# Two softmax attentions of a five-stage kernel: scores in groups of 32 rows, turns in two halves, one bank for q, k and v, norms by four tiles, mask by sixteen

## The chip, the cores and the metric

The kernel runs on one NeuronCore of a Trainium2 chip. Its time is the device time of one launch in microseconds. Before the change the median of three runs is 3300.31 us (3300.05 to 3302.07). The engines are PE (matrix multiply, with its weight loads shown apart as PEld), DVE (VectorE), ACT (ScalarE), POOL (GpSimd) and SP, which issues most DMAs.

## The reference

The input x is 128 sequences of 64 tokens of width 128, with a context of the same shape. A stack of four gated cross-attention blocks follows, each with a feed-forward; all data is float32. The change touches two of the attentions, both multi-head softmax attentions with 16 heads of width 8:

```
x^ = layernorm(x);  q = x^ Wq + bq;  k = ctx Wk + bk;  v = ctx Wv + bv
scores[h] = q[h] k[h]^T / sqrt(8)          64 x 64 per sequence and head
layer 1 alone: padded keys and keys after the query are masked out
x = x + (softmax(scores) v) Wo + bias
```

The others (a lag-correlation attention, a retention, integer, gated and expert-routed feed-forwards and attentions) are left as they are.

## The kernel before

Two sequences make a tile of 128 tokens, so there are 64 tiles. x stays in SBUF as X[128, 64, 128], and the transposed context as CT. `program` runs the stages one after another: weights; the first attention with its feed-forward; `softmax_attention` for layer 1; the next feed-forward; retention; the gated feed-forward; `softmax_attention` for layer 3, which also stores x to DRAM; and last the expert-routed stage (`switch_attention`), which takes more than half of the time and is not touched.

Inside `softmax_attention` each engine has its own instruction list, written out for all tiles by `straight(stages, bufs)`: at step t every stage (lag, function) works on tile t - lag, in the order of the list. That order is the engine's program order, and semaphores hold the engines together. SBUF buffers rotate over NS = 4 tiles; the eight PSUM banks do not rotate, so each is written again only when it was read. A tile passes through these steps:

- DVE takes the moments of its 128 rows (L217, L220), adds epsilon (L223); POOL raises to the power -1/2 (L236); DVE normalises (L244, `norm`).
- PE turns x (`turn_x`, L1165), ACT keeps it (L1088). PE projects q, k and v (`project`, L1150 to L1155): q and k in one bank, v in another. ACT keeps q and k with their biases (L1079, L1082). DVE spreads v over a block-wise layout (`widen` of DVE, L1043).
- POOL spreads the key (`widen` of POOL, L985): with 16 heads of 8 rows, `key_wide` holds for each of 8 heads of a half the key with all other heads' rows set to zero. So one matmul with 64 contraction rows gives the scores of 8 heads: 64 queries by 8 x 64 keys.
- PE makes the scores (`scores`, L1139): 2 halves of heads by 2 sequences are four matmuls of 64 rows, 64 columns and 512 moving columns, two banks in all.
- Layer 1: DVE builds the tile's mask row (L1016), adds it to the scores (L1022), takes the row maximum (L1031), and POOL subtracts it (`centre`, L979). Layer 3: DVE takes the maximum straight from PSUM (L1026) and subtracts it (L1036).
- ACT exponentiates (L1073). PE turns the probabilities (`turn_probs`, L1129), eight transposes into two banks; ACT keeps them in one instruction (L1069). PE weighs the values (`weigh`, L1118), DVE divides by the row sum (L1006, L1010), PE turns the heads (L1107), ACT keeps them, PE makes the output (L1100), and DVE adds it to x (L1002).

PE's list is: turn heads, output, project, turn probabilities, weigh, turn x, scores. SP fetches the tile's context from CT into a buffer of four (L956), SBUF to SBUF, and in layer 3 stores x (L960). In layer 1 SP first loads the causal mask and the padding mask, and DVE waits for both before anything else but four small copies.

## Time and profile before

| what | value |
|---|---|
| median of the runs | 3300.31 us |
| the profiled execution, its own time | 3297.7 us |
| its span, first to last instruction | 3295.9 us |
| mean granted TensorE clock | 0.923 |
| busy share of PE, DVE, ACT, POOL | 89%, 85%, 71%, 70% |
| layer 1's attention, first to last instruction | about 233 to 561 us |
| layer 3's attention | about 1010 to 1325 us |
| expert-routed stage with its weights | from about 1327 us to the end |

The busy shares are means over stages with different limits. The page's slices give the outline, the busy times of chosen stretches tell which engine is full in each, and the timeline of one step tells why. A matmul in float32 leaves two records.

### The profile page before, as it was taken

The numbers are of one execution on the slowest core, as the hardware profiler recorded it, in microseconds if no ns is written. First come the engines' busy times: TensorE is split into PE (matmuls) and PEld (weight loads), VectorE is DVE, ScalarE is ACT, GpSimd is POOL, SyncE is SP. The second block draws the span as 40 slices with busy tenths as digits, with TensorE's granted clock in tenths as the row PEclk, the third lists the DMA queues.
The fourth block names the chain that finished last, engine by engine and source line by source line (L and its number), as shares of the span: only waits on it lengthen the run. The fifth ranks groups of instructions, "written<-read, shape, count | busy, mean of one in ns | idle before, by whom it ended". The sixth has DMA issues, their size and how long they took to land.

```text
span 3295.9 us, 78554 instructions
## 1 busy us (share of the span) xinstructions
PE 2947.3 (89%) x24633; PEld 2207.1 (67%) x24646; DVE 2792.6 (85%) x9096; ACT 2344.1 (71%) x7533; POOL 2305.8 (70%) x3108
## 2 busy tenths in 40 slices
PE   6639997289668999399999999999999999999998
PEld 6526775167345777277777777777777777777776
DVE  4369997599897998588999989898989999898987
ACT  3276665777896666477777777777777777777776
POOL 1179996564686665167777777777777777777777
PEclk8559998599678999699999999999999999999999
DMA  3000000022000100400000000000000000000000
GB/s 111 15 12 16 16 17 7 21 73 71 1 1 21 31 29 27 124 8 8 7 9 9 8 7 9 9 8 9 7 8 9 7 7 8 9 8 7 8 8 5
DMA packets 132959, 63.73 MB, mean 19 GB/s; under 512 B 20417, under 2 KB 132161, under 8 KB 132545
## 3 DMA queue, kind: packets, MB, share of 16 engines
q1 hardware_dynamic: 132544, 58.70, 6.4%
q8 instruction: 200, 3.28, 0.4%
q14 instruction: 215, 1.75, 0.2%
HBM read 41.82 MB, written 8.45 MB: 15 GB/s over the span
## 4 chain that ended last, share of the span: by engine, by line
PE 57%; POOL 0%; DVE 0%; ACT 0%; issue 0%; DMA 0%; POOLq 0%; SPq 0%; DVEq 0%; ACTq 0%
PE ps_sw_a L2127 23%; PE ps_sw_d L2127 22%; PE ps_sw_w L2169 4%; PE ps_sw_w L2156 3%; PE ps_sw_s L2142 2%; PE ps_sw_s L2180 2%; PE ps_sw_m L2147 1%; PE ps_sw_m L2135 0%; ACT sw_scaled L1915 0%; POOL sw_o_rest L1881 0%; POOL sw_o_rest L1878 0%; DVE sw_v_part L2029 0%; ACT sw_probs L1964 0%; DMA sw_x<-scratch_x 0%; DVE sw_r_sel L2044 0%
## 5 line engine op out<-in xcount | busy, mean ns | idle before, releaser
L1915 ACT ACTIVATE sw_scaled<-ps_sw_a,sw_gate_o 128x128 f32<-128x128 f32 x2048 | 620.5, 447 | 252.3 <-PE ps_sw_a L2127 244.3
L1915 ACT ACTIVATE sw_scaled<-ps_sw_a,sw_gate_v 128x128 f32<-128x128 f32 x2048 | 597.7, 450 | 203.3 <-PE ps_sw_a L2127 203.2
L2029 DVE SCALAR_TENSOR_TENSOR sw_o_part<-ps_sw_d,sw_gate_o,sw_o_part 128x128 f32<-128x128 f32 x1920 | 555.1, 338 | 60.6 <-PE ps_sw_d L2127 59.5
L1854 POOL TENSOR_TENSOR sw_v_pair<-sw_v_part,sw_scaled 128x256 f32<-128x256 f32 x512 | 378.2, 739 | 158.8 <-DVE sw_v_part L2029 101.7
L2029 DVE SCALAR_TENSOR_TENSOR sw_v_part<-ps_sw_d,sw_gate_v,sw_scaled 128x128 f32<-128x128 f32 x1024 | 304.8, 338 | 123.1 <-PE ps_sw_d L2127 104.3
L1878 POOL TENSOR_TENSOR sw_o_rest<-sw_o_rest,sw_scaled 128x256 f32<-128x256 f32 x384 | 285.3, 743 | 155.2 <-ACT sw_scaled L1915 117.9
L2029 DVE SCALAR_TENSOR_TENSOR sw_v_part<-ps_sw_d,sw_gate_v,sw_v_part 128x128 f32<-128x128 f32 x1024 | 304.5, 338 | 0.0
L1881 POOL TENSOR_TENSOR sw_o_rest<-sw_o_rest,sw_scaled 128x256 f32<-128x256 f32 x384 | 282.7, 736 | 30.1
L1859 POOL TENSOR_TENSOR sw_v<-sw_v_pair 128x128 f32<-128x128 f32 x512 | 241.7, 472 | 40.1
L985 POOL TENSOR_TENSOR at_key_wide<-at_keyT,c_half_heads 128x1024 f32<-128x1024 f32 x128 | 242.5, 1895 | 4.2 <-ACT at_keyT L1082 4.2
L2127 PE MATMUL ps_sw_a<-sw_v_high,sw_xT_high 128*128 128x512 f32 x512 | 235.6, 460 | 0.4 <-ACT sw_scaled L1915 0.3
L2127 PE MATMUL ps_sw_a<-sw_o_high,sw_ctx_high 128*128 128x512 f32 x512 | 214.6, 419 | 0.6 <-ACT sw_scaled L1915 0.6
L2127 PE MATMUL ps_sw_d<-sw_v_high,sw_xT_high 128*128 128x512 f32 x512 | 208.0, 406 | 0.0
L2127 PE MATMUL ps_sw_d<-sw_o_high,sw_ctx_high 128*128 128x512 f32 x512 | 207.2, 405 | 0.0
L2127 PE MATMUL ps_sw_d<-sw_v_low,sw_xT_high 128*128 128x512 f32 x512 | 203.0, 396 | 0.0
L2127 PE MATMUL ps_sw_a<-sw_v_low,sw_xT_high 128*128 128x512 f32 x512 | 202.7, 396 | 0.0
L2127 PE MATMUL ps_sw_a<-sw_v_high,sw_xT_low 128*128 128x512 f32 x512 | 202.3, 395 | 0.0
L2127 PE MATMUL ps_sw_d<-sw_v_high,sw_xT_low 128*128 128x512 f32 x512 | 201.9, 394 | 0.0
L2127 PE MATMUL ps_sw_a<-sw_o_low,sw_ctx_high 128*128 128x512 f32 x512 | 201.8, 394 | 0.0
L2127 PE MATMUL ps_sw_d<-sw_o_low,sw_ctx_high 128*128 128x512 f32 x512 | 201.5, 393 | 0.0
L2127 PE MATMUL ps_sw_a<-sw_o_high,sw_ctx_low 128*128 128x512 f32 x512 | 200.3, 391 | 0.0
L2127 PE MATMUL ps_sw_d<-sw_o_high,sw_ctx_low 128*128 128x512 f32 x512 | 200.3, 391 | 0.0
(326 smaller groups left out, 8582.1 us busy)
## 6 DMA issues: line engine op xcount, KB each, us to landing
at_ctxT<-ctx_T SPq DMA_DIRECT2D x128, 64.0 KB, 1.8
re_values<-in_ctx SPq DMA_DIRECT2D x128, 64.0 KB, 2.4
x<-in_x SPq DMA_DIRECT2D x16, 256.0 KB, 3.4
l_ctx<-in_ctx SPq DMA_DIRECT2D x16, 256.0 KB, 3.0
re_ctx<-in_ctx SPq DMA_DIRECT2D x16, 256.0 KB, 3.1
scratch_x<-x SPq DMA_DIRECT2D x64, 64.0 KB, 1.8
swp_staged<-in_L_ffn_v_w SPq DMA_DIRECT2D x8, 512.0 KB, 5.9
swp_staged<-in_L_ffn_o_w SPq DMA_DIRECT2D x8, 512.0 KB, 7.1
```

What stands on the lines that cost most here:

```text
L985: pool.tensor_tensor(key_wide[:, s], keyT[:, s].unsqueeze(1).broadcast_to([P, HALF, P]), C["half_heads"][:].unsqueeze(2).broadcast_to([P, ...
L1854: pool.tensor_tensor(v_pair[:, h % 2], v_part[:, h], scaled[:, h % 4, 2:4], ALU.add)\
L1859: pool.tensor_tensor(v[:, h], v_pair[:, h % 2, 0], v_pair[:, h % 2, 1], ALU.add).then_inc(q["v"], 1)
L1878: pool.tensor_tensor(o_rest[:, 0:2], o_rest[:, 0:2], scaled[:, h % 4, 0:2], ALU.add)\
L1881: pool.tensor_tensor(o_rest[:, 2:4], o_rest[:, 2:4], scaled[:, h % 4, 2:4], ALU.add)\
L1915: act.activation(scaled[:, h % 4, e], ps_a[h % 2][:, e], ACT.Copy, scale=gates[:, s, h, HALF_E + e:HALF_E + e + 1]).then_inc(a_scaled[kind ...
L2029: dve.scalar_tensor_tensor(out=acc[:, e % 2], in0=ps_d[h % 2][:, e], scalar=gates[:, s, h, e:e + 1], in1=before, op0=ALU.mult, op1=ALU.add ...
L2127: m = pe.matmul(bank, lhs[a], w[b][:, h, experts], start=c == 0, stop=c == 2)
L2142: m = pe.matmul(ps_s[t, h], probs[t, s, h], C["ident"][t, t], start=True, stop=True)
L2156: m = pe.matmul(ps_w[n][:, h * P:(h + 1) * P], W["pair"][:, 4 * n + h], xT[:, s], start=True, stop=True)
L2169: m = pe.matmul(ps_w[b][:, h * S:(h + 1) * S], v[t, h], probs_T[t, h], start=True, stop=True)
L2180: m = pe.matmul(ps_s[t], xT[:, s, t], uT[:, :, t], start=True, stop=True)
```

## The change

`softmax_attention` is written anew in these points, for both layers; the retention is not changed.

- A new constant `quarter_heads`; `key_wide` holds 4 heads' keys in place of 8. Scores are eight matmuls of 32 rows, 64 columns and 256 moving columns. Each group of 32 rows has a bank of its own, half used, so scores take four banks.
- The probabilities are turned in two halves of four transposes through one bank: first half, `weigh` of the tile before, second half. ACT keeps each half with its own instruction.
- q, k and v share one bank; DVE places the values after the key was kept.
- The norm's small steps are done once for four tiles, and the normalisation is an ACT instruction with scale and bias.
- The mask of layer 1 is built for 16 tiles at a time, and only that step waits for the masks' loads.
- The context is read from CT directly, and its fetches are gone.
- Lags grow by five steps for scores and what follows them.

```diff
-    for name, shape in (("ident", [P, P]), ("half_heads", [P, HEADS // 2]), ("half_mask", [P, 2])):
+    for name, shape in (("ident", [P, P]), ("half_heads", [P, HEADS // 2]),
+                        ("quarter_heads", [P, HEADS // 4]), ("half_mask", [P, 2])):
...
-        ctxT = k.sb(name + "_ctxT", [P, NS, P])
-        key_wide = k.sb(name + "_key_wide", [P, NS, HALF, P])
+        key_wide = k.sb(name + "_key_wide", [P, NS, QUARTER, P])
-        ps_s = k.psum(name + "_scores", [P, HEADS, S])
-        ps_t = k.psum(name + "_turned", [P, HALF, P])
+        ps_s = k.psum(name + "_scores", [P, 4, 512])[:, :, 0:QUARTER * S].rearrange("p r (j s) -> p r j s", j=QUARTER)
+        ps_t = k.psum(name + "_turned", [P, HALF // 2, P])
         ps_a = k.psum(name + "_a", [P, 2, P])
-        ps_qk = k.psum(name + "_qk", [P, 2, P])
-        ps_v = k.psum(name + "_v", [P, P])
+        ps_qkv = k.psum(name + "_qkv", [P, 3, P])
+        ps_v = ps_qkv[:, 2]
...
-                def fetch(i, s, r):
-                    if not first(i, NS):
-                        sp.wait_ge(q["proj"], i - NS + 1)
-                    sp.dma_start(ctxT[:, s], tile_of(CT, i)).then_inc(ctx_in[s], 16)
... POOL
-                stages = [(5, centre)] if masked else []
-                straight(stages + [(1, add_bias), (0, rstd), (3, widen)], NS)
+                stages = [(10, centre)] if masked else []
+                straight(stages + [(7, add_bias), (1, by_group(rstd)), (8, widen)], NS)
... DVE
-                if masked:
-                    dve.wait_ge(q["consts"], 48)
+                def build_mask(i, s, r):
+                    if i % CHUNK == 0:
+                        if i == 0:
+                            dve.wait_ge(q["consts"], 48)
+                        dve.scalar_tensor_tensor(out=mask[:, i:i + CHUNK], in0=padding[:, i:i + CHUNK], scalar=NEG,
+                                                 in1=causal[:].unsqueeze(1).broadcast_to([P, CHUNK, S]),
+                                                 op0=ALU.mult, op1=ALU.min).then_inc(q["mask"], 1)
...
+                def place_values(i, s, r):
                     dve.wait_ge(q["proj"], i + 1)
+                    dve.wait_ge(q["keyT"], i + 1)
...
+                def negated_mean(g, s):
+                    dve.wait_ge(q["rstd"], g + 1)
+                    if g >= 4:
+                        dve.wait_ge(q["xhat"], N * (g - 3))
+                    dve.scalar_tensor_tensor(out=small["nmr"][:, s], in0=mv[:, s, :, 0], scalar=-1.0, in1=small["rstd"][:, s],
+                                             op0=ALU.mult, op1=ALU.mult).then_inc(q["nmr"], 1)
...
-                straight([(5, read_scores), (9, final), (5, centre), (1, norm), (0, front), (3, widen), (7, normalise)], NS)
+                stages = [(10, read_scores), (14, final), (10, centre), (2, by_group(negated_mean)), (0, moments),
+                          (1, aggregate), (1, by_group(variance)), (8, place_values), (12, normalise)]
+                straight(([(7, build_mask)] if masked else []) + stages, NS)
... ACT
+                def norm(i, s, r):
+                    act.wait_ge(q["nmr"], i // N + 1)
...
+                    act.activation(xhat[:, s], X[:, i], ACT.Identity, bias=small["nmr"][:, g, i % N:i % N + 1],
+                                   scale=small["rstd"][:, g, i % N:i % N + 1]).then_inc(q["xhat"], 1)
...
-                straight([(8, keep_heads), (3, keep_q), (6, keep_probs), (2, keep_x), (5, exp)], NS)
+                straight([(13, keep_heads), (8, keep_q), (11, keep_probs(0)), (6, norm), (11, keep_probs(1)), (7, keep_x),
+                          (10, exp)], NS)
... PE
-                    for half in range(2):
-                        h = slice(half * S, (half + 1) * S)
-                        for b in range(2):
-                            t = slice(b * S, (b + 1) * S)
-                            m = pe.matmul(ps_s[t, half * HALF:(half + 1) * HALF], qT[h, s, t], key_wide[h, s, :, t],
-                                          start=True, stop=True)
+                    for b in range(2):
+                        t = slice(b * S, (b + 1) * S)
+                        for quarter in range(4):
+                            h = slice(quarter * ROWS, (quarter + 1) * ROWS)
+                            m = pe.matmul(ps_s[t, quarter], qT[h, s, t], key_wide[h, s, :, t], start=True, stop=True)
...
-                straight([(8, turn_heads), (9, output), (3, project), (6, turn_probs), (7, weigh), (2, turn_x),
-                               (4, scores)], NS)
+                straight([(13, turn_heads), (14, output), (8, project), (11, turn_probs(0)), (12, weigh), (11, turn_probs(1)),
+                          (7, turn_x), (9, scores)], NS)
```

## Rows read from the trace of the kernel before

**Rows 1.** The page: PE's busy share in 40 equal slices, in tenths.

```profile
PE   6639997289668999399999999999999999999998
```

**Rows 2.** Stretches of layer 1 and 3: length, each engine's busy us, clock, DMA.

```profile
core 0: us, PE busy (x) PEld busy (x) DVE busy (x) ACT busy (x) POOL busy (x), PEclk, DMA share, GB/s
249.00:544.00 295.00, 290.89 (x3939) 206.26 (x3935) 282.81 (x671) 194.13 (x370) 290.95 (x247) 0.99 0.05 15
1018.50:1311.00 292.50, 290.71 (x3940) 207.00 (x3943) 261.86 (x609) 194.97 (x373) 178.15 (x184) 0.99 0.10 29
```

**Rows 3.** Timeline of a step of layer 3: start, us, engine, line, operation.

```profile
...
1149.80 1.23 DVE L1026 TENSOR_REDUCE at_top<-ps_at_scores 128x16 f32<-128x1024 f32 x1 [0.31 <-PE ps_at_scores L1139]
...
1150.98 1.09 PE L1129 MATMUL ps_at_turned<-c_ident,at_probs 128*128 128x128 f32 x8
...
1151.38 0.36 ACT L1082 ACTIVATE at_keyT<-ps_at_qk,w_bk 128x128 f32<-128x128 f32 x1
...
1152.27 0.34 DVE L244 TENSOR_SCALAR at_xhat<-x,at_mv,at_rstd 128x128 f32<-128x128 f32 x1
...
1153.06 0.15 DVE L223 TENSOR_SCALAR at_var<-at_mv 128x1 f32<-128x1 f32 x1
...
1153.31 1.09 PE L1139 MATMUL ps_at_scores<-at_key_wide,at_qT 64*64 64x512 f32 x8
...
1153.81 1.90 POOL L985 TENSOR_TENSOR at_key_wide<-at_keyT,c_half_heads 128x1024 f32<-128x1024 f32 x1
1153.86 0.29 DVE L1010 TENSOR_TENSOR at_heads_out<-ps_at_o,at_rsum 128x128 f32<-128x128 f32 x1
...
1154.33 0.33 PE L1107 MATMUL ps_at_a<-c_ident,at_heads_out 128*128 128x128 f32 x1
...
1154.46 1.23 DVE L1026 TENSOR_REDUCE at_top<-ps_at_scores 128x16 f32<-128x1024 f32 x1 [0.31 <-PE ps_at_scores L1139]
```

**Rows 4.** Timeline of a step of layer 1.

```profile
...
400.02 0.14 PEld L1107 LDWEIGHTS ps_at_a<-c_ident,at_heads_out 128*128 128x128 f32 x1 [0.81 <-DVE at_heads_out L1010]
...
400.33 1.23 DVE L1022 TENSOR_TENSOR at_raw<-ps_at_scores,at_mask 128x1024 f32<-128x1024 f32 x1
...
401.67 1.21 DVE L1031 TENSOR_REDUCE at_top<-at_raw 128x16 f32<-128x1024 f32 x1
...
402.97 1.93 POOL L979 TENSOR_TENSOR at_probs<-at_raw,at_top 128x1024 f32<-128x1024 f32 x1
...
404.70 0.14 PEld L1107 LDWEIGHTS ps_at_a<-c_ident,at_heads_out 128*128 128x128 f32 x1 [0.81 <-DVE at_heads_out L1010]
...
406.04 1.09 PE L1129 MATMUL ps_at_turned<-c_ident,at_probs 128*128 128x128 f32 x8
```

**Rows 5.** Timeline in retention: its score matmuls and the load behind them.

```profile
...
705.24 1.11 PE L1404 MATMUL ps_re_s<-re_q_wide,re_kT 64*64 64x256 f32 x16
...
706.27 1.01 PEld L1389 LDWEIGHTS ps_re_o<-re_val_wide,re_probs 128*64 128x64 f32 x32 [0.39 <-issue]
```

**Rows 6.** Single tiles of other stages: line, count: ns min/median/max, first and last start.

```profile
L1349 ACT ACTIVATE re_xhat<-x,re_nmr,re_rstd x64: 477/481/495, 647.6 to 800.2; 128x128 f32<-128x128 f32 x64
L1296 DVE SCALAR_TENSOR_TENSOR re_nmr<-re_mv,re_rstd x16: 794/1366/1643, 646.8 to 797.5; 128x4 f32<-128x4 f32 x16
...
L1272 POOL TENSOR_TENSOR re_rstd<-re_var,minus_half x16: 1017/1017/1019, 645.7 to 796.1; 128x4 f32<-128x4 f32 x16
...
L321 DVE SCALAR_TENSOR_TENSOR l_nmr<-l_mv,l_rstd x16: 151/162/164, 39.8 to 101.7; 128x4 f32<-128x4 f32 x16
...
L372 ACT ACTIVATE l_xT<-ps_l_x x16: 572/597/597, 44.1 to 112.4; 128x512 f32<-128x512 f32 x16
```

**Rows 7.** The mask row of layer 1, all 64, in the same view.

```profile
L1016 DVE SCALAR_TENSOR_TENSOR at_mask<-at_padding,at_causal x64: 214/476/1004, 249.4 to 544.3; 128x64 f32<-128x64 uint8 x64
```

**Rows 8.** Timeline: the kernel's start and the start of layer 1.

```profile
...
2.58 0.43 SPq L164 DMA_DIRECT2D gates_raw<-in_g_ffn  x1
...
240.44 0.29 DVE L217 BATCH_NORM_STATS2 at_stats<-x 128x6 f32<-128x128 f32 x1 [7.18 <-DMA at_padding<-in_mask_BxS_bf]
...
248.65 1.99 PE L1139 MATMUL ps_at_scores<-at_key_wide,at_qT 64*64 64x512 f32 x8
```

More of the change, by code:

```diff
@@ L938, in softmax_attention, with by_group, at, by_rows @@
         out_ps = ps_o[:, 256:256 + D]
-        q = k.sems(name, *LN_SEMS, "consts", "ctx_read", "x_turned", "xT", "proj", "qT", "keyT", "key", "val", "ones",
-                   "scores", "mask", "masked", "top", "centred", "exp", "p_turned", "p_kept", "pv", "rsum",
-                   "heads", "h_turned", "h_kept", "out", "x", "biased", "stored")
-        ctx_in = [k.sem(f"{name}_ctx_in{n}") for n in range(NS)]
+        q = k.sems(name, "stats", "moments", "var_eps", "rstd", "nmr", "xhat", "consts", "x_turned", "xT", "proj", "qT", "keyT",
+                   "key", "val", "ones", "scores", "mask", "masked", "top", "centred", "exp", "p_turned", "p_kept", "pv",
+                   "rsum", "heads", "h_turned", "h_kept", "out", "x", "biased", "stored")
+        def by_group(step):
+            def at(i, s, r):
+                if i % N == N - 1:
+                    step(i // N, i // N % 4)
+            return at
+        def by_rows(ap):
+            return ap.rearrange("p (r j) s -> p r j s", r=4)
+        def head_wide(ap):
+            return ap.rearrange("p (r j) -> p r j", r=4).unsqueeze(3).broadcast_to([P, 4, QUARTER, S])
         with nc.Block() as block:
@@ L961, in store @@
                         .then_inc(q["stored"], 16)
-                straight([(0, fetch)] + ([(10, store)] if out is not None else []), NS)
                 if out is not None:
+                    straight([(0, store)], NS)
                     sp.wait_ge(q["stored"], 16 * TILES)
@@ L976, in centre @@
                     pool.wait_ge(q["top"], i + 1)
-                    if not first(i, NS):
-                        pool.wait_ge(q["p_turned"], i - NS + 1)
+                    if i >= NS:
+                        pool.wait_ge(q["p_turned"], 2 * (i - NS + 1))
                     pool.tensor_tensor(probs[:, s], raw[:, s], top[:, s].unsqueeze(2).broadcast_to([P, HEADS, S]),
@@ L1007, in normalise @@
                     dve.wait_ge(q["rsum"], i + 1)
-                    if not first(i, NS):
+                    if i >= NS:
                         dve.wait_ge(q["h_turned"], i - NS + 1)
@@ L1109, in weigh @@
                 def weigh(i, s, r):
-                    pe.wait_ge(q["p_kept"], i + 1)
+                    pe.wait_ge(q["p_kept"], 2 * i + 2)
                     pe.wait_ge(q["val"], i + 1)
-                    if not first(i, 2):
+                    if i >= 2:
                         pe.wait_ge(q["x"], i - 1)
@@ L1122, in weigh, with turn_probs, step @@
                     m.then_inc(q["pv"], 1)
[L1124 to L1140 removed]
+                def turn_probs(part):
+                    def step(i, s, r):
+                        pe.wait_ge(q["exp"], i + 1)
+                        if 2 * i + part:
+                            pe.wait_ge(q["p_kept"], 2 * i + part)
+                        for n in range(HALF // 2):
+                            j = part * HALF // 2 + n
+                            m = pe.transpose(ps_t[:, n], probs[:, s, 2 * j:2 * j + 2].rearrange("p h k -> p (h k)"),
+                                             C["ident"][:])
+                        m.then_inc(q["p_turned"], 1)
+                    return step
+                def scores(i, s, r):
+                    pe.wait_ge(q["key"], i + 1)
+                    pe.wait_ge(q["qT"], i + 1)
+                    if i:
+                        pe.wait_ge(q["masked" if masked else "centred"], i)
+                    for b in range(2):
[3 more added lines that the diff above has]
+                            m = pe.matmul(ps_s[t, quarter], qT[h, s, t], key_wide[h, s, :, t], start=True, stop=True)
                     m.then_inc(q["scores"], 1)
@@ L1144, in project @@
                     pe.wait_ge(q["xT"], i + 1)
-                    pe.wait_ge(ctx_in[s], 16 * r + 16)
-                    if not first(i, 1):
+                    if i:
                         pe.wait_ge(q["qT"], i)
@@ L1149, in project @@
                         pe.wait_ge(q["val"], i)
-                    pe.matmul(ps_qk[:, 0], W["q"][:], xT[:, s], start=True, stop=True)
-                    pe.matmul(ps_qk[:, 1], W["k"][:], ctxT[:, s], start=True, stop=True)
+                    pe.matmul(ps_qkv[:, 0], W["q"][:], xT[:, s], start=True, stop=True)
+                    pe.matmul(ps_qkv[:, 1], W["k"][:], CT[:, i], start=True, stop=True)
                     for parity in range(2):
```

124 lines of the change are left out of this document (66 added, 58 removed).

## The prediction

> **What bounds the kernel now.** The page of the profile comes first: its slices say that PE is full in two stretches which are no part of the last stage, the fourth to sixth slice and the fourteenth to sixteenth [rows 1]. The code puts the softmax attentions of layers 1 and 3 there. The stretches' busy times confirm it: PE 98.6% and 99.4% at the full clock (0.99 of 2.4 GHz), and in layer 1 DVE is at 96% and POOL at 99% too [rows 2]. ACT is at 66%. Then one step of the timeline for each attention, since a step repeats unchanged some 60 times.
>
> Layer 3 [rows 3]: DVE's row maximum starts at 1149.80 and again at 1154.46, so a step is 4.66 us. PE runs without a gap: the turns of the probabilities at 1150.98, scores at 1153.31, next turn of heads at 1154.33. Scores occupy it 1.02 us. DVE begins 0.13 us after PE's scores make way (1154.46 against 1154.33) and ends its last operation at 1153.86 + 0.29 = 1154.15, before PE wants it. PE alone sets this step.
>
> Layer 1 [rows 4]: 404.70 - 400.02 = 4.68 us. Here three bounds meet. PE has the same work. DVE has no gap. And there is a chain: scores read at 400.33, centred by POOL from 402.97, turned on PE at 406.04, which is 5.71 us from the read to the turn and crosses a step.
>
> **The change part by part.** I call the step of layer 3 T3, that of layer 1 T1, and count 61 steady steps of each (64 tiles less filling).
>
> Scores. Four matmuls of 64 rows, 64 columns and 512 moving columns become eight of 32 rows and 256 columns. One matmul is two records of about 0.61 us; four quadrants go side by side and the whole takes 1.02 us. The trace has no 32-row tile. The nearest rows are retention's: 64x64 tiles, 256 columns, 16 records from 705.24 to the next load at 706.27, so 1.03 us for eight matmuls, four at a time [rows 5]. Upper bound 1.03 if no more than four run together, lower bound half of it, 0.51, if eight do. I take 0.51 plus 0.1 for eight more records to issue, 0.61, since four and two column halves already share the array here and only the number of row groups is new. PE's step becomes 4.66 - 1.02 + 0.61 = 4.25 us.
> The Trainium skill, TensorEngine Tiling (Array Packing), lists 32x64 among its modes with eight tiles, under Tiling Modes. The same page, Performance Considerations, warns that tiling speeds up TensorE and not PSUM's evacuation. By the one, 0.51; by the other the readers of PSUM are next, which is where the following terms end up.
>
> Key widening on POOL: half the elements. It is 1.90 us for 1024 now [rows 3]. Between a half (0.95) and all of it I take 1.04, the half and some fixed cost. In layer 3 it is hidden (POOL is busy 178 of 292 us [rows 2]). In layer 1 it takes POOL off its bound: about 4.62 a step, less 0.86, less the grouped power.
>
> Norms by four tiles. DVE loses the normalisation (0.34, of which 0.3 is not overlapped) and the one-column addition (0.15) [rows 3]. Per group it gets an addition (0.15 again) and the negated mean (0.16 alone [rows 6]). POOL's power, now once a tile, becomes 1.02 per four tiles [rows 6]. ACT gets the normalisation at 0.48 [rows 6]. DVE in layer 3: 1154.15 - 1149.80 = 4.35, less 0.45, makes 3.90; with 0.13 of semaphore at each end 4.16, under PE's 4.25, so it hides, with only 0.09 to spare. In the group's step it is 4.16 + 0.31 = 4.47, plus what the negated mean waits for POOL. In retention this instruction takes 1.37 us in the median against 0.16 elsewhere [rows 6]: it reads two SBUF tensors while POOL works. In layer 3 POOL's widening (1.04) runs from about 2.1 to 3.1 us of the step and the negated mean arrives at 2.6, so 0.5 more at worst. That is 0.22 to 0.72 lost per four steps; with a step of every four I take 0.4, or 0.10 a tile. T3 = 4.35.
>
> Turns in two halves, one bank. PE's work is the same eight transposes. The second half waits for ACT to clear the first, and `weigh` of the tile before lies between, about 1.0 us (2.33 from the turns' start to scores, less the turns' 1.0 and the turn of x, 0.3 [rows 3]). An eviction of 512 columns is 0.60 us [rows 6], so two are 1.20 in place of 1.02. ACT takes query and key first, the key from 1151.38 to 1151.74 or 2.1 us into PE's step (which began at 1149.67, 4.66 before 1154.33) [rows 3], then the half until 2.6; PE asks at 1.3 + 0.5 + 1.0 = 2.8 or a little later. The cover is 0.2 to 0.3 us; gone, every step pays what it lacks. Behind the waiting turn stand turn of x and scores. ACT in all: 195 / 292.5 x 4.66 = 3.1, plus 0.48, plus 0.18 = 3.8, under the step.
>
> q, k and v in one bank, with values placed after the key is kept: DVE reaches the values at about 3 us, the key is kept at 2.1, so it costs nothing. The fetch DMAs go and with them a transfer per tile on SP's queue. PE has no gap in the step that could be a wait for one, so this too is worth nothing.
>
> The chain of layer 1. DVE no longer builds a mask row between, so the read starts 0.13 after PE's scores and not 0.31. Read to turn stays 5.71. From the turn to the end of scores PE needs 1153.31 - 1150.98 = 2.33 plus 0.61. The loop spans two steps: (0.13 + 5.71 + 2.33 + 0.61) / 2 = 4.39. This is later than PE's 4.25, so the chain through POOL's centring is what is late next. With 0.04 for group steps T1 = 4.43.
>
> Mask by sixteen. It was 0.48 per tile in the median, 0.21 at least and 1.00 at most [rows 7]: again two SBUF inputs against POOL. 1024 elements at the rate of DVE's other 1024 forms is 1.2 us; at the worst, in proportion to 0.21 for 64, it is 3.4. Three of the four chunks fall into steady steps and stand before the read of scores. With a wait for POOL's operation, 1.3 each, 4 us in all; bounds 0 and 10.
>
> Filling. In layer 1 DVE waited 7.18 us for the padding mask before its first statistics at 240.44 (0.29 each) [rows 8]. Now statistics begin at once and only the mask at lag 7 waits. Five statistics steps of 0.5, the power 1.0, norm, turn, project and the wait for the constants until 240.4, then the mask's 1.2: first scores near 244.2, where they were at 248.65 [rows 8]. Gain 4.4. In layer 3 there was no such wait and the five steps cost about 3, against 1.9 saved by the smaller widening and the lost stalls: 0.6 later. Draining through two half turns costs 0.5 in layer 1, nothing sure in layer 3. One more constant on SP's queue: 0.47 between issues (last at 2.58 [rows 8]), ahead of everything: 0.5.
>
> **The sum.** Layer 3: 61 x (4.66 - 4.35) = 18.9, less 0.6, 18.3. Layer 1: 61 x (4.68 - 4.43) = 15.3, less 4, plus 4.4, less 0.5, 15.2. Constants -0.5. Together 33.0 us. The profiled execution took 3297.7 (span 3295.9) and would take 3264.7; the median shown is 2.6 above it, so 3267.3.
>
> **The rivals.** About 0.2%, 6.6 us, is what can be told from no change here.
> (B) Better: the group step's excess is absorbed and eight tiles cost 0.51. T3 = 4.20, T1 = 4.36: 9 + 4 more, 3254. For it: DVE's operations overlap by nearly 0.1 each. Against: only 0.09 of slack.
> (C) No more than four matmuls run at once, as retention's rows show for eight: scores 1.03, both steps stay near 4.67 and only the ends count: 0.6 - 0.6 + 4.4 - 4 - 0.5 - 0.6 - 0.5, about 3302. Retention's tiles are limited to four by shape, so they don't decide it.
> (D) The negated mean loses to POOL's centring in layer 1. Both wait for the row maximum. If POOL is first, DVE stands for 1.93: that group step is 4.16 + 0.31 + 1.93 = 6.4, 2.0 over, 0.5 a tile, T1 = 4.93. Layer 1 then loses 15.3 + 0.1, layer 3 with 1.04 of wait per group (T3 = 4.48) gains 10.4: 3306. It decides from a wait of about 1 us on. For it: retention's 1.37. Against: DVE issues it behind its own maximum, with no semaphore between, and POOL starts 0.09 later (402.97 against 401.67 + 1.21 [rows 4]).
> The Trainium skill, SBUF — State Buffer, section on its two separate sides, calls this pair of ports an exclusive lock held for the whole instruction by the first to start. The retention row agrees (0.79 to 1.64 against 0.16), and by it the result hangs on who is first, as in (D).
> (E) The other side: the four row groups don't run beside each other, only the two column halves. Then four rounds of 0.51 are 2.04, PE's step is 5.68, and 2 x 61 x 1.02 = 124 us are added: 3425. It decides as soon as scores pass 1.1 us. Against: two row groups do run together in both traces' rows.
>
> **Chances.** Forecast 0.66, B 0.14, C 0.07, D 0.08, E 0.05. Faster by over 0.2%: forecast, B and a mild D, 0.82. Within 0.2%: half of C and D, 0.09. Slower 0.09. The range leaves out E, the worst of D and C and the best of B: 3248 to 3298, where the unknown costs (scores 0.51 to 1.03, mask 0 to 10, group steps 0.22 to 0.72) put most of their weight.
>
> **What would show it.** Scores: 16 records of 32 rows in about 0.6 us, next turn of heads 4.25 to 4.4 later. DVE without idle time in layer 3. In layer 1 ACT's exponential following POOL's centring at once, and PE waiting for it at the first half turn. Negated mean under 0.7 us in the median. First scores of layer 1 near 244. The prediction is wrong if PE idles at the second half turn (the cover was not there), if scores take over 0.8, or if the mask chunks take over 2 us.

## The result

The changed kernel takes 3308.14 us (median of 12 runs, 3303.77 to 3312.29) against 3300.33 us before (12 runs, 3290.80 to 3304.69). The ratio is 1.0023, with a 95% interval from 1.0016 to 1.0031. The forecast was 3267.3 with a range up to 3298: it was wrong in sign and outside its range. The profiled execution has a span of 3305.2 us, 9.3 more than before, where the prediction's own sum was 33.0 less.

The page's slices, then the busy times of the two stretches in the profile after (they answer to [rows 1] and [rows 2]):

```profile
PE   6649997289667999499999999999999999999998
...
249.00:544.00 295.00, 270.88 (x4316) 207.94 (x4315) 249.92 (x499) 213.64 (x482) 218.55 (x198) 0.97 0.01 2
1018.50:1311.00 292.50, 275.62 (x4358) 211.10 (x4359) 237.59 (x511) 210.16 (x494) 107.38 (x143) 0.96 0.05 15
```

No engine is full now. In layer 3 PE falls from 290.7 to 275.6 us of 292.5, DVE from 261.9 to 237.6, POOL from 178.2 to 107.4. The work did shrink as forecast, and the time didn't: it has turned into waits. The timeline of one step tells which. Layer 3, PE from one scores to the next, and then the two copies of ACT on which PE's wait hangs (they answer to [rows 3]; columns as there):

```profile
...
1165.30 0.66 PE L1179 MATMUL ps_at_turned<-c_ident,at_probs 128*128 128x128 f32 x4
1165.79 0.27 PE L1217 MATMUL ps_at_a<-c_ident,at_xhat 128*128 128x128 f32 x1
1166.00 0.69 PE L1193 MATMUL ps_at_scores<-at_key_wide,at_qT 32*64 32x256 f32 x16
1166.90 0.30 PE L1155 MATMUL ps_at_a<-c_ident,at_heads_out 128*128 128x128 f32 x1 [0.22 <-ACT at_xT L1135]
```

```profile
...
1165.99 0.60 ACT L1114 ACTIVATE at_probs_T<-ps_at_turned 128x512 f32<-128x512 f32 x1 [0.65 <-PE ps_at_turned L1179]
1166.49 0.27 ACT L1135 ACTIVATE at_xT<-ps_at_a 128x128 f32<-128x128 f32 x1
```

The turn of heads starts 0.90 us after the scores and not 0.61, because it waits for the copy of the turned x. `turn_heads` has always had that wait in the code (both turns use one bank). Before, ACT copied x right after its turn, under scores of 1.02 us (they ran from 1153.31 to 1154.33 [rows 3]):

```profile
...
1153.42 0.28 ACT L1088 ACTIVATE at_xT<-ps_at_a 128x128 f32<-128x128 f32 x1 [0.28 <-PE ps_at_a L1165]
```

Now ACT takes the second half of the turned probabilities first (`straight([... keep_probs(1)), (7, keep_x) ...])`), stands for it until 1165.99, and gives x only at 1166.76, while scores have become short. The steps in layer 3 are 4.59 us, with 4.75 to 4.77 in nine of them. This is **cause B** below.

In layer 1 three steps of four are 4.59 too; the fourth is 5.29. DVE's part of such a step:

```profile
...
321.38 0.17 DVE L1082 BATCH_NORM_AGGREGATE at_mv<-at_stats 128x2 f32<-128x6 f32 x1
321.58 1.69 DVE L1086 TENSOR_SCALAR at_var<-at_mv 128x4 f32<-128x4 f32 x1
323.19 0.41 DVE L1065 TENSOR_TENSOR at_val_wide<-ps_at_qkv,c_half_mask 128x256 f32<-128x256 f32 x1
...
323.80 0.29 DVE L1032 TENSOR_TENSOR at_heads_out<-ps_at_o,at_rsum 128x128 f32<-128x128 f32 x1
```

GpSimd's centring in that step, and PE:

```profile
...
321.35 1.90 POOL L994 TENSOR_TENSOR at_probs<-at_raw,at_top 128x1024 f32<-128x1024 f32 x1 [0.79 <-DVE at_top L1052]
```

```profile
...
322.62 0.69 PE L1193 MATMUL ps_at_scores<-at_key_wide,at_qT 32*64 32x256 f32 x16
324.14 0.33 PE L1155 MATMUL ps_at_a<-c_ident,at_heads_out 128*128 128x128 f32 x1 [0.84 <-DVE at_heads_out L1032]
```

The group's addition of epsilon over four columns lasts 1.69 us, until GpSimd's centring ends (323.27 and 323.25). The values, the reciprocal and the division of the heads stand behind it in DVE's list, and PE idles 0.84 us. The group's small operations in all steady steps, layer 1 first, then layer 3 (line, count: ns min/median/max):

```profile
L1086 DVE TENSOR_SCALAR at_var<-at_mv x14: 1689/1689/1881, 261.9 to 513.1; 128x4 f32<-128x4 f32 x14
...
L1074 DVE SCALAR_TENSOR_TENSOR at_nmr<-at_mv,at_rstd x14: 149/152/154, 268.5 to 518.2; 128x4 f32<-128x4 f32 x14
...
L1086 DVE TENSOR_SCALAR at_var<-at_mv x13: 169/170/171, 1058.7 to 1280.3; 128x4 f32<-128x4 f32 x13
...
L1074 DVE SCALAR_TENSOR_TENSOR at_nmr<-at_mv,at_rstd x14: 151/893/922, 1044.5 to 1284.7; 128x4 f32<-128x4 f32 x14
```

Where POOL centres (layer 1) the addition meets it; where POOL only widens (layer 3) the negated mean does, 0.89 us. This is **cause A**.

The start of layer 1 (answers to [rows 8]):

```profile
...
243.23 1.23 DVE L1017 SCALAR_TENSOR_TENSOR at_mask<-at_padding,at_causal 128x1024 f32<-128x1024 uint8 x1 [4.91 <-DMA at_padding<-in_mask_BxS_bf]
...
249.11 1.22 DVE L1042 TENSOR_TENSOR at_raw<-ps_at_scores,at_mask 128x1024 f32<-128x1024 f32 x1 [0.39 <-PE ps_at_scores L1193]
```

The first scores are read 1.67 us earlier than before (250.78), not 3.9. The 9.3 us can be split by the starts of the first and last reads of the scores in both traces: first read of layer 1 -1.7; first to last read in layer 1 294.5 before, 302.9 after, +8.4; on to layer 3's first +0.1; layer 3 291.7 and 291.4, -0.3; the rest +2.7. Forecast were -3.9, -11.3, +1.1, -18.9 and 0. The stretches from first to last read in the two attentions are 38 of the 42 us missed.

### The profile page after: what moved, and what is told of

The parts are those of the page before. It is cut to its first block, busy times and chain, and to the rows that moved or that the text cites. A ratio compares the mean times of both kernels' runs of the same rounds, so it can differ in the third digit from the quotient of the medians.

```text
span 3305.2 us, 80565 instructions
## 1 busy us (share of the span) xinstructions
PE 2922.3 (88%) x25657; PEld 2217.5 (67%) x25670; DVE 2738.2 (83%) x8844; ACT 2392.9 (72%) x7789; POOL 2165.4 (66%) x3012
## 4 chain that ended last, share of the span: by engine, by line
PE 57%; DVE 0%; POOL 0%; ACT 0%; issue 0%; DMA 0%; POOLq 0%; SPq 0%; DVEq 0%; ACTq 0%
PE ps_sw_a L2179 23%; PE ps_sw_d L2179 22%; PE ps_sw_w L2221 4%; PE ps_sw_w L2208 3%; PE ps_sw_s L2194 2%; PE ps_sw_s L2232 2%; PE ps_sw_m L2199 1%; PE ps_sw_m L2187 0%; ACT sw_scaled L1967 0%; DVE sw_v_part L2081 0%; POOL sw_o_rest L1930 0%; POOL sw_o_rest L1933 0%; ACT sw_probs L2016 0%; DMA sw_x<-scratch_x 0%; DVE sw_r_p L2091 0%
## 5 line engine op out<-in xcount | busy, mean ns | idle before, releaser
L1114 ACT ACTIVATE at_probs_T<-ps_at_turned 128x512 f32<-128x512 f32 x256 | 152.9, 597 | 96.9 <-PE ps_at_turned L1179 96.8
L1001 POOL TENSOR_TENSOR at_key_wide<-at_keyT,c_quarter_heads 128x512 f32<-128x512 f32 x128 | 133.2, 1041 | 129.9 <-ACT at_keyT L1129 129.9
```

Of the source, the lines that this page charges most:

```text
L1001: pool.tensor_tensor(key_wide[:, s], keyT[:, s].unsqueeze(1).broadcast_to([P, QUARTER, P]), C["quarter_heads"][:].unsqueeze(2).broadcast_t ...
L1114: act.activation(probs_T[:, s, part * HALF // 2:(part + 1) * HALF // 2], ps_t, ACT.Copy)\
```

## The experiments

Each was timed over five rounds beside the kernel before; ratios are to it, and that of the change is 1.0023. "Layer 1 goes at" and "layer 3 goes at" give the steps from one read of the scores to the next. "4.26/4.53" means that the two alternate.

**1. The epsilon addition at the end of DVE's list.**

```
-                          (1, aggregate), (1, by_group(variance)), (8, place_values), (12, normalise)]
+                          (1, aggregate), (8, place_values), (12, normalise), (1, by_group(variance))]
```

> One edit to the changed kernel: the group's addition of epsilon on DVE (variance) moves from behind the moments to the end of DVE's list. Theory A: in layer 1 this 4-column addition takes 1.70 us because it waits until POOL's centring ends, and it makes every fourth step 5.29 in place of 4.59. At the end of the list it starts about 0.3 to 0.5 us before the centring ends, so it lasts 0.3 to 0.6 us and ends beside DVE's own wait for scores: steps of 5.29 go down to at most 4.75, layer 1 is 8 us shorter (13 x 0.6), layer 3 at most 2 us; total about 3299. Rival: the long step comes from the group's other work (POOL's power of four columns before the widening); then steps stay at 5.29 and the time at 3308.

3300.19 us, 0.9999 (0.9988 to 1.0011), 8 us under the change. Layer 1 goes at 4.59 from its sixth step on, apart from the mask's steps; layer 3 stays at 4.59/4.77. The addition there:

```profile
L1086 DVE TENSOR_SCALAR at_var<-at_mv x14: 159/388/405, 261.9 to 507.6; 128x4 f32<-128x4 f32 x14
```

Cause A is shown, with its price: 13 steps by 0.70 is 9 us. From first to last read layer 1 is only 4.9 us shorter (298.0 against 302.9): in this trace PE's lower clock lasted longer at the start of the layer (granted 0.50 in place of 0.57 from 255 to 270 us), and the fourth and fifth step took 7.12 and 5.78 us in place of 4.84 and 4.59.

**2. The turn of x ahead of the weighing, its copy ahead of the norm.**

```
-                straight([..., (11, turn_probs(0)), (12, weigh), (11, turn_probs(1)), (7, turn_x), (9, scores)], NS)
+                straight([..., (11, turn_probs(0)), (7, turn_x), (12, weigh), (11, turn_probs(1)), (9, scores)], NS)
-                straight([..., (11, keep_probs(0)), (6, norm), (11, keep_probs(1)), (7, keep_x), (10, exp)], NS)
+                straight([..., (11, keep_probs(0)), (7, keep_x), (6, norm), (11, keep_probs(1)), (10, exp)], NS)
```

> One edit to the changed kernel, order alone: PE turns x before it weighs the values (not after the second half turn), and ACT keeps x before the norm and the second half (not after it). Theory B: PE's next turn of heads waits 0.3 us for ACT's copy of x, which stands behind the 0.60 copy of the second half; scores themselves free PE after about 0.6. Then the gap from the scores' start to the next turn of heads falls from 0.90 to 0.6 to 0.65 and the step from 4.59 to about 4.35 unless DVE's values (which wait for the weighing) hold it at 4.45: 122 x 0.14 to 0.24 = 17 to 29 us less, so 3279 to 3291 with group steps unchanged. Rival B2: scores in 32-row tiles occupy PE for 0.9 whatever stands behind them (a switch of tile shape); then the gap stays 0.9 and the time 3308.

3282.70 us, 0.9948 (0.9936 to 0.9961). PE in layer 3:

```profile
...
1164.27 0.69 PE L1193 MATMUL ps_at_scores<-at_key_wide,at_qT 32*64 32x256 f32 x16
1164.89 0.33 PE L1155 MATMUL ps_at_a<-c_ident,at_heads_out 128*128 128x128 f32 x1
```

The wait is gone and scores occupy PE 0.62 us. Layer 3 goes at 4.26, with 4.36 in every fourth: 272.0 us from first to last read in place of 291.4. Layer 1 keeps its 5.28, and three of its steps last 6.07 to 6.11: PE's clock falls there (last section).

**3. Both.** The two edits above together.

> Both edits of the two others together. If A and B are right and independent: 3308 less 8 to 10, less 17 to 29, so 3269 to 3283. If DVE becomes the bound once PE doesn't wait, the sum is smaller than the parts. Rivals as with the two.

3276.78 us, 0.9924 (0.9912 to 0.9937). Layer 1 alternates between 4.26 and 4.53, mean 4.40, where the prediction's chain gave 4.39. But layer 3 worsens to steps of 4.26 to 4.36 with 4.60 in every fourth, mean 4.38: a late addition makes POOL's power late, its widening slides under the negated mean, and that takes 0.89 us each time (0.56 in experiment 2).

**4. The same by layer**: the addition last in layer 1 alone (`if masked`), the early x in both.

> Both moves by layer: the turn of x before the weighing and its copy before the second half of the weights' copies in both layers; the group's epsilon addition last on VectorE in layer 1 alone. Theory (two separate causes, each in its own layer): layer 3 keeps the steps of 4.26 with 4.36 every fourth that it had with the early turn alone, layer 1 the 4.26/4.53 that it had with both moves, so the kernel gives 3276.8 - 64 x (4.41 - 4.31) = about 3270 us. Rival (the late addition doesn't cost layer 3 its 0.1 us a step; something else drifts): the time stays at 3277, and layer 3 shows 4.6 in some steps all the same.

3265.71 us, 0.9894 (0.9878 to 0.9909). It is the fastest of all kernels here, and within 2 us of the forecast. Layer 1 at 4.26/4.53, layer 3 at 4.26/4.36.

**5. Only ACT's list**: `(6, norm), (7, keep_x), (11, keep_probs(1))`, PE's order as in the change.

> Only ScalarE's list is changed: the copy of the turned x goes ahead of the copy of the second half of the turned weights; TensorE's order stays as in the change. Theory (the wait is one of order on ScalarE, not of TensorE's work): turn heads no longer waits 0.22 us, the stretch from the scores' start to it falls from 0.90 to some 0.62 to 0.7, and the layer-3 step from 4.59 to 4.3 to 4.4; but x is turned on TensorE after the second half of the weights, so that its copy now delays that half's copy by a wait for TensorE. If that wait takes the place, layer 3 stays at 4.5 to 4.6 and the time within 3300 to 3308; if the order on ScalarE alone was the matter, about 3283 to 3290. Rival (turn heads is late for TensorE's own reasons, the 32-row scores occupying it for 0.9): no change, 3308, with 0.90 from scores to turn heads.

3284.84 us, 0.9943 (0.9926 to 0.9960). ACT in layer 3:

```profile
...
1161.90 0.28 ACT L1135 ACTIVATE at_xT<-ps_at_a 128x128 f32<-128x128 f32 x1 [0.77 <-PE ps_at_a L1217]
1162.07 0.59 ACT L1114 ACTIVATE at_probs_T<-ps_at_turned 128x512 f32<-128x512 f32 x1
```

The turn of heads is at 1162.41, 0.62 after the scores at 1161.79, and the step 4.26. So cause B is the order of two entries in ACT's list: the second half may wait, x may not.

**6. Scores back to 64 rows in two banks**, with the widening of 1024 elements; the rest as in the change.

```
-                            m = pe.matmul(ps_s[t, quarter], qT[h, s, t], key_wide[h, s, :, t], start=True, stop=True)
+                            m = pe.matmul(ps_8[t, half * HALF:(half + 1) * HALF], qT[h, s, t], key_wide[h, s, :, t],
+                                          start=True, stop=True)
```

> The changed kernel with scores as before: four matmuls of 64 rows and 512 columns in two banks, key widened to 8 heads (1024 elements on POOL), all else of the change kept. By theory B most of the shorter scores are lost in the wait for x's copy, so longer scores fill it: scores' start to next turn of heads 1.02 in place of 0.90, step 4.71 in place of 4.59 in layer 3, 61 x 0.12 = 7 us more there. In layer 1 POOL has 0.86 more work a step (4.4 us of 4.7): same or up to 0.3 a step more. Total 3315 to 3335. Rival (scores occupy PE 0.9 by themselves): the same 0.12, this run doesn't tell it apart; it prices the part. If instead the time falls below 3300, the 32-row tiles themselves are what costs.

3325.78 us, 1.0076 (1.0064 to 1.0089). So the scores' part, with its shorter widening, is worth 17.6 us inside the change, and all other parts together cost 25 against the kernel before. Layer 3 has 4.66 with a pair of 4.93 and 4.96 in every four. One of the group's steps, POOL first, then DVE:

```profile
...
1171.83 1.90 POOL L1002 TENSOR_TENSOR at_key_wide<-at_keyT,c_half_heads 128x1024 f32<-128x1024 f32 x1 [0.26 <-ACT at_keyT L1130]
```

```profile
...
1172.28 1.46 DVE L1075 SCALAR_TENSOR_TENSOR at_nmr<-at_mv,at_rstd 128x4 f32<-128x4 f32 x1
```

The negated mean ends with the widening (1173.73 and 1173.74).

**7. And besides the turns in one piece** (eight transposes, one copy, on top of 6).

> The kernel with 64-row scores in two banks (3325.8 us), and besides the weights are turned in one piece of eight transposes and copied in one instruction, as before the change. Theory (the halves bring a second wait on ScalarE that the turned x stands behind; in one piece the copy of x follows its turn again): the layer-3 steps of 4.93/4.96 in every fourth become 4.66, and the time goes down to 3310 to 3318. Rival (the loss of that kernel against the one before comes from the norms by group and not from the halves): 3322 to 3330, with the 4.9 steps still there.

3321.12 us, 1.0065 (1.0050 to 1.0080), between the two ranges and next to the rival's; the interval overlaps with that of 6, and the 4.92/4.96 are still there. So the halves are not what makes the long steps. That the norms by group do is read from the rows of 6 (1.46 us for the negated mean, 1.69 for the addition in layer 1); no run has long scores without the grouping. Halves against the whole is not settled beyond "within 5 us".

**8. The norms tile by tile**, on top of 2 (epsilon, power and normalising each step, the last on DVE).

> With the early turn of x, the norms go tile by tile as before the change (epsilon addition, power and normalising each step, the normalising on VectorE, 0.481 us); all else as in the change. Theory (VectorE needs the relief of the grouping once TensorE is at 4.25): VectorE carries 3.84 us a step in layer 3 after the change and would carry 3.84 + 0.48 + some 0.25 = 4.55, so layer 3 goes at 4.55 instead of 4.29 (+16 us), layer 1 at 4.6 to 4.7 instead of 4.67 (about 0): 3295 to 3302. Rival (the grouping costs by its own waits what it saves): layer 3 stays at 4.3 to 4.4 and layer 1 goes at 4.4 to 4.5, since the four-column addition that waited for GpSimd is gone: 3268 to 3278.

3274.42 us, 0.9926 (0.9905 to 0.9946). DVE carries 13.7 us more in layer 3 than in experiment 2 (226.7 against 213.0 of the 240 us from 1045), and layer 3 goes at 4.40 (4.28/4.52) and not at 4.55, layer 1 at 4.42 to 4.44. The additions of one column in layer 1:

```profile
L225 DVE TENSOR_SCALAR at_var<-at_mv x57: 152/153/156, 267.8 to 521.6; 128x1 f32<-128x1 f32 x57
```

The rival holds for the sum: grouping as the change does it costs more in waits than it saves (8 us by the medians, with intervals that overlap). The steps say where. In layer 1 the grouping loses (285.5 us from first to last read without it, 299.4 with it, or 297.0 in experiment 5), in layer 3 it gains (4.40 a step without it, 4.29 with it). With the addition last in layer 1 (experiment 4) it gains in both: 281.2 us in layer 1 and 4.29 a step in layer 3.

**9. The mask one tile at a time**, on top of 4: `CHUNK = 1`.

> The kernel of both moves by layer, with the mask built tile by tile (64 additions of 64 columns) instead of sixteen tiles at a time (4 of 1024 columns); TensorE, ScalarE and GpSimd keep their lists. Theory (the mask by sixteen is worth little here, since VectorE has 0.5 us a step free in layer 1: it carries 231.9 us of 278): one more VectorE instruction of 0.2 us a step, hidden, while the three long steps of 14.3 instead of 13.1 us that the chunks bring fall away: 0 to 4 us faster, 3262 to 3266. Rival (as the prediction took it: the mask by sixteen saves VectorE time on the step's path, 4 us in all): 3268 to 3275, layer-1 steps over 4.40.

3275.35 us, 0.9923 (0.9909 to 0.9936), 10 us over experiment 4 by the medians and 3.7 by the spans of the profiled executions. Layer 1 goes at 4.52, with 4.59 in every fourth, where the other alternates between 4.26 and 4.53; from first to last read it takes 286.2 us against 281.2. The mask and the centring that holds it:

```profile
...
329.31 1.90 POOL L994 TENSOR_TENSOR at_probs<-at_raw,at_top 128x1024 f32<-128x1024 f32 x1 [1.20 <-DVE at_top L1052]
...
330.63 0.67 DVE L1017 SCALAR_TENSOR_TENSOR at_mask<-at_padding,at_causal 128x64 f32<-128x64 uint8 x1
...
331.22 1.21 DVE L1042 TENSOR_TENSOR at_raw<-ps_at_scores,at_mask 128x1024 f32<-128x1024 f32 x1
```

My theory (hidden) fell. 64 columns need 0.19 us (the fastest of the 64) and take 0.67 at the median, ending with the centring. Beside the mended lists the mask by sixteen is worth 5.0 us in layer 1. (The prediction's 4 us, which the rival calls a saving, were the cost of the four chunks.)

**10. Mask later, values in eight buffers**, on top of 4: `(9, build_mask)` and `val_wide` eight deep.

> As the kernel with both moves by layer, and besides: the mask is built two places later in VectorE's list (lag 9 instead of 7), and the widened values have eight buffers instead of four. Theory (the slow filling of layer 1 comes from the mask's wait for the padding's transfer, 4.9 us, ahead of the first values on VectorE): the first values and the first four steps come 2 to 4 us earlier, so 2 to 4 us less than the kernel of both moves by layer, all of it ahead of 300 us in the trace. Rival (the filling is set by the halves' handshake at the half clock, not by the mask): no difference, within 1 us.

3269.33 us, 0.9899 (0.9883 to 0.9915): no gain, as the rival had it, but not for its reason. The first scores are read at 241.80 in place of 248.22. Of these 6.4 us the stage ahead, which has the same code, accounts for 4.1 (its last matmuls start at 223.70 and 227.82), so the edit is worth 2.3 there, inside the theory's 2 to 4. Behind the first step the next four are 6.11, 7.01, 7.11 and 5.82, in place of 6.49, 4.72, 4.14 and 4.58, and the last read is at 530.37 against 529.43. The stretches from 240 and from 255 us, experiment 4 first, then this one (columns as in [rows 2]):

```profile
240.00:255.00 15.00, 10.26 (x82) 6.53 (x78) 10.04 (x21) 5.11 (x16) 7.71 (x8) 0.50 0.08 5
255.00:270.00 15.00, 14.18 (x212) 10.50 (x211) 10.19 (x21) 11.10 (x26) 10.51 (x11) 0.85 0.01 3
```

```profile
240.00:255.00 15.00, 13.31 (x112) 8.65 (x111) 11.01 (x20) 7.62 (x21) 9.77 (x9) 0.50 0.00 1
255.00:270.00 15.00, 15.00 (x168) 11.41 (x166) 7.54 (x17) 7.42 (x18) 8.46 (x8) 0.53 0.01 2
```

PE is full from 255 to 270 and does 168 matmul records where the other does 212, since it works at its lower level (1.2 of 2.4 GHz) for longer. That need not come from the edit. Experiments 2 and 11 differ in one instruction alone, read their first scores at 246.78 and 246.49, and were granted 0.87 and 0.61 from 255 to 270 us (third and fourth step 5.22 and 4.47 against 7.01 and 5.58). So one profile of each doesn't show whether the early start or chance made the clock rise later, and the edit's worth is not settled.

**11. The addition in another form**, at its place, on top of 2.

```
-                    dve.tensor_scalar(small["var"][:, s], mv[:, s, :, 1], EPS, None, ALU.add).then_inc(...)
+                    dve.scalar_tensor_tensor(out=small["var"][:, s], in0=mv[:, s, :, 1], scalar=EPS, in1=mv[:, s, :, 1],
+                                             op0=ALU.add, op1=ALU.max).then_inc(...)
```

> With the early turn of x; the group's epsilon addition stays at its place in VectorE's list, but is written as a two-operation instruction on two tensor operands, max(var + epsilon, var), over the same four columns, in place of the tensor-and-scalar form. Theory (it is this form on four strided columns that stands still while GpSimd's centring runs; the negated mean, two tensor operands and four columns, took 0.154 us at the median, and the one-column tensor-and-scalar form 0.15 us beside a centring): the addition takes about 0.16 us, layer 1 goes at 4.26/4.53 (4.40 mean) and layer 3 at 4.26/4.36 (4.29): 3282.7 - 64 x (4.67 - 4.40) = about 3266 us. Rival (the place is the matter, four strided columns wait for GpSimd in any form): the addition stays at 1.7 us, steps of 5.28 in every fourth, 3283 us.

3285.31 us, 0.9955 (0.9940 to 0.9970): the theory of the form fell. Its premise was weak: the negated mean, which has this form too, already stood for 0.89 us beside the widening in layer 3.

```profile
L1086 DVE SCALAR_TENSOR_TENSOR at_var<-at_mv x13: 1681/1683/1876, 280.5 to 509.8; 128x4 f32<-128x4 f32 x13
```

**12. Neighbouring columns**: `mv` as `[P, 4, 2, N]`, on top of 2.

> With the early turn of x and the epsilon addition at its place; the group's means and variances are kept as four means and then four variances, so that the addition reads four neighbouring columns instead of every second one (the aggregation writes its two results four columns apart instead). Theory (four-column operations of VectorE stand still while GpSimd runs a centring or a widening, however their columns lie): the addition stays at 1.68 to 1.70 us, a step of 5.28 in every fourth of layer 1, 3279 to 3286 us. Rival (it is the reading of every second column that waits): 0.16 us, layer 1 at 4.40, 3264 to 3270 us.

3284.39 us, 0.9955 (0.9939 to 0.9972), the addition at 1684/1686/1881 ns. The stride isn't it.

**13. Three columns and one**, on top of 2.

> With the early turn of x; the group's epsilon addition at its place, split into an addition over three columns and one over the fourth. Theory (more than one column is what waits for GpSimd: one column took 0.15 us beside a centring, four took 1.69): the three columns take 1.6 to 1.7 us and the single one 0.15 or less, the time is that of the early turn alone, 3282 to 3288 us. Rival (an even number of columns is what waits): both take about 0.15 us, layer 1 goes at 4.40 and the time is 3264 to 3270 us.

3289.59 us, 0.9968 (0.9956 to 0.9981), 1.6 us above the theory's range; the long steps are 5.34 in place of 5.28.

```profile
L1086 DVE TENSOR_SCALAR at_var<-at_mv x14: 1686/1688/1883, 264.4 to 514.2; 128x3 f32<-128x3 f32 x14
L1087 DVE TENSOR_SCALAR at_var<-at_mv x14: 138/140/141, 266.0 to 516.0; 128x1 f32<-128x1 f32 x14
```

The three columns wait. The single one stands behind them and starts as the centring ends, so it says nothing on a wait; experiment 14 does.

**14. Four single columns**, at the same place, on top of 2.

```
+                    for n in range(N):
+                        m = dve.tensor_scalar(small["var"][:, s, n:n + 1], mv[:, s, n:n + 1, 1], EPS, None, ALU.add)
+                    m.then_inc(q["var_eps"], 1)
```

> With the early turn of x; the group's epsilon addition at its place, written as four additions of one column each. Theory (a one-column addition doesn't wait for GpSimd, as before the change): four instructions of 0.15 us or less, 0.3 to 0.5 us in all in place of 1.69; layer 1 goes at 4.26/4.53 with some 0.1 to 0.3 more in every fourth step (mean 4.43 to 4.47), layer 3 as with the early turn alone (4.29 to 4.35): 3282.7 - 64 x (4.67 - 4.45) = about 3269, from 3264 to 3274. Rival (it is the place in the list, where the centring is always running, and the old one-column addition only stood elsewhere): the first of the four takes 1.6 us, no gain, 3282 to 3288 us.

3273.32 us, 0.9906 (0.9890 to 0.9922); layer 1 at 4.26/4.53, layer 3 at 4.26/4.36. All four together:

```profile
...
338.08 0.34 DVE L1087 TENSOR_SCALAR at_var<-at_mv 128x1 f32<-128x1 f32 x4
```

The centring runs from 337.84 to 339.74, all around them, and 56 of the kernel's single-column additions in layer 1 lie inside a centring, at 0.142 to 0.155 us. This closes cause A: at one place in the list, four columns or three wait, and one column does not. Four instructions are five times as fast as one. From first to last read both layers are as long as in experiment 4 (281.6 and 272.3 us against 281.2 and 271.9).

## Why the prediction was wrong

**Scores, widening, normalisation, power: right.** Scores: forecast 0.61, measured 0.62 (experiment 2). The sixteen records start in two groups of eight, 0.27 us apart, where retention's start in fours. The widening was forecast at 1.04 and takes 1.04, the power 1.02, ACT's normalisation 0.48.

**Turns in two halves: the step that failed in layer 3.** The prediction gave this part no cost. It followed the second half to PE ("Behind the waiting turn stand turn of x and scores") and found the cover of 0.2 to 0.3 us sufficient. In steady steps PE indeed doesn't idle there. What it didn't follow was the same wait on ACT: `keep_probs(1)` waits for PE, and `keep_x` is queued behind it. Nor did it list `turn_heads`' wait for x, since in the trace of before that wait never shows: x was copied under the 1.02 us of scores. Shortening the scores took away the cover and the halves made the copy late, both in one change. It costs 0.28 to 0.33 in every step: 19.4 us in layer 3 (291.4 against 272.0), all of the gain forecast there. With the two entries turned round, the mean step of 4.29 lies between the forecast's 4.35 and rival B's 4.20.

**Norms by four: the step that failed in layer 1.** Rival D priced the right mechanism for the wrong instruction. The negated mean issues right behind the row maximum and beats the centring, as argued (0.152 at the median). The addition of epsilon, taken at "0.15 again", comes 0.23 us after the centring has started (321.58 against 321.35) and stands till its end: 1.69 us. The one-column addition at 0.154 in the trace of before lay inside a centring 59 times of 64 in layer 1 and didn't wait; it was read as the price of the four-column one, and it is just the one that doesn't wait. In layer 3 the term "0.5 more at worst" was 0.40 beyond 0.16 once the steps were short (0.56) and 0.73 in the change (0.89). The Trainium skill, SBUF — State Buffer, section "Who interferes with whom", lists a tensor-and-scalar operation within SBUF among those that can take the pair of ports shared with GpSimd; the prediction had used that page for the negated mean alone. The Trainium skill, VectorE: DVE Perf Modes, section "What auto-detection actually checks", ties the mode in which this happens to the dimensions that are larger than one. Experiments 13 and 14 agree: 1.69 us at three columns (three and three are equal, which that section allows), 0.14 at one beside a centring.

**The chain of layer 1: right, but covered.** 4.39 was forecast and 4.40 measured, once both causes are gone. The chain shows in experiment 4's rows: in every second steady step PE waits 0.20 us for ACT's exponential. Causes A and B overlap there. By the steady steps, taking away B alone gains 0.10 us a step (experiment 5), A alone 0.17 (experiment 1), both 0.37 (experiment 4). From first to last read this is 5.9, 4.9 and 21.7 us, with the longer time at the lower clock in experiment 1's.

**Mask by sixteen: the size in its frame.** The chunks take 1.44 us at the median, and the two steps at each take 0.45 us more than two others (5.54 and 4.09), 1.4 us in the change; in experiment 4 the three there take 1.0 more, 3 us in all. Forecast were 4, from 0 to 10. Against one tile at a time the chunks gain 5.0 us in layer 1 (experiment 9).

**q, k and v in one bank, context without a fetch: nothing against it.** In the steady steps no wait on either shows in PE's or DVE's rows. At the start of layer 1 PE stands 4.2 us for the first values before it projects the next tile, and those stand behind the mask (next paragraph). Neither part was tested alone.

**Filling: too hopeful by about 2 us.** The first scores start at 247.85 and not 244.2. Of these 3.65 us, 1.8 come from the stage ahead: its code is the same, and its last matmuls start at 228.69 in place of 226.90. The rest is the place of the mask: the first values stand behind it on DVE, and it waits 4.91 us for the padding. Putting the mask later, with more buffers, brought 2.3 us back (experiment 10). Between the layers +1.1 was forecast and +0.1 came. Layer 3's filling was not tested. The +2.7 behind the last read is not explained either; its code is the same, and in the traces here this stretch lasts from 1983.3 to 1988.2 us.

**The sum.** Of the 42 us between forecast and trace, 38 lie in the two attentions, and mending causes A and B brings back 41.2 there (21.7 and 19.5, experiment 4). With both mended by order alone, in the lists of DVE, ACT and PE, the kernel takes 3265.7, 1.6 under the forecast. The closeness is in part luck, as errors of either sign cancel: 2.0 and 0.9 us better than forecast in the attentions, 1.3 and 1.8 worse at the start of layer 1 and behind the last read. That is no excuse for the forecast: the lists were there to be read. None of its signs of being wrong points at either cause: in steady steps PE doesn't idle at the second half turn, scores keep PE for 0.6 by themselves, and the chunks stay under 2 us. Of what was to show the forecast right, the negated mean is over its 0.7 in layer 3 (0.89 at the median). Rival D's time (3306) lies near the result by luck: it had layer 1 lose 15.4 us and layer 3 gain 10.4, and the trace has a loss of 8.4 and a gain of 0.3. A small DVE operation that stands for the centring was in it, but the wrong one, and it didn't have cause B.

## What to carry to other kernels

When an operation on the bottleneck is shortened, list every wait of the instruction right behind it, also those that never show in the trace, and ask for each whether it was hidden under the part that goes. When one instruction is cut in two, follow both engines' lists: what stands behind the new second wait is delayed even where the waiting engine has time. Beside a long GpSimd operation on SBUF, look at every small VectorE operation and not only at the one that showed the stall: put it where GpSimd is idle, differently by stage if need be, or split it into single columns.

## What was not expected of the hardware

- An addition over three or four columns within SBUF took 1.68 to 1.69 us beside GpSimd's running centring and ended with it, whether its columns were neighbours or not and in the form with two inputs too; one over a single column at the same place took 0.14. Statistics over 128 columns and their aggregation didn't wait: 0.29 and 0.18 us beside a centring, in experiment 8.
- Eight matmuls of 32 rows (sixteen records) took 0.62 us where four of 64 rows with twice the columns (eight records) took 1.02.
- In the stalled steps of layer 1 PE's clock fell now and then, once cause B was gone and the idle time of PE in them had grown from 0.84 to 1.27 us: in ten of some fifty such steps in experiments 2, 5 and 11 to 13, and in none of the change. In experiment 12, at 433 us, after 1.27 us of idle PE, the matmuls of the projections took 0.64 us in place of 0.39, and that step 6.07 us in place of 4.60. What sets the ten apart from the others is not settled.
